# Two key tiles at a time: the TensorE order in the first attention of a four-layer cross-attention kernel

## The chip, the cores and the metric

The kernel runs on one core of one Trainium2 chip. The metric is the device time of one execution in microseconds (us). Before the change it is 2722.48 us, the median of three runs (2721.83 to 2725.4).

## The reference

The program works on a batch of 4 sequences of 256 tokens by 256 features, with a context of 1601 rows by 128 features for each, in four layers: a gated cross-attention with a feed-forward part, a memory layer, a block with self-attention, cross-attention and an expert MLP, and a second memory layer. The change lies in the attention of the first layer, for each of the 4 sequences and 16 heads of width 64:

```
q = (layernorm(x) @ Wq) * 64 ** -0.5          # 256 x 64 for a head
k, v = split(media @ Wkv)                     # 1601 x 64 for a head
sim = where(mask, q @ k.T, -big)              # 256 x 1601
out = softmax(sim) @ v
```

## The kernel before

The kernel is written by hand: every engine has its own program, and semaphores order them. Nothing is scheduled by a planner. An engine takes its instructions strictly in the order of the text, so the order in which the TensorE code is written is the order on the engine.

**The first attention.** Heads are taken in pairs (`p`, 8 pairs for a sequence, called steps here), and keys in 13 tiles of 128 (`kt`, padded from 1601 to 1664). The steps run in a loop that is unrolled twice (steps 0 to 5), with steps 6 and 7 written behind it. In one step TensorE does for each key tile:

- *scores*: four matmuls of 256 columns into a PSUM bank `st` (two banks, taken in turn by `kt % 2`), transposed: keys on the partitions, 2 heads x 256 queries on the free axis. Their operands are high and low halves of float32 numbers (`q_hi_hi`, `k_hi_lo`, `q_lo_shift`, `k_hi_rows`). The scores of tile `kt` wait for the exponential of tile `kt - 2`, which frees the bank (`p_exp`).
- *a maximum part*, `max_part`: softmax needs the maximum of each query over all keys before its scores are computed. For the *next* pair it is taken in 8 parts (2 halves of the keys x 2 heads x 2 query tiles), each two matmuls of 416 columns into PSUM tile `x` (two buffers, `n % 2`). Part `n` waits until VectorE has reduced part `n - 2` (`max_read`). The parts stand at `kt` 2 to 9. The last step of a sequence has no next pair and no parts.
- *the value product*, `pv(kt)`: `v` times the exponentials, for the two heads in the two halves of the array's columns (64 columns each, out of `probs`, into PSUM `pv`). It waits for the exponential of its tile, and it runs two tiles behind the scores.

ScalarE computes the exponentials out of `st` into one of four `probs` buffers (L508). It may write a buffer when the value product and the sums of four tiles before have read it. GpSimd adds the even tiles' exponentials into `prob_sums` (L427 for the first two, L431 for the others), VectorE the odd ones (L1137), both from SBUF. VectorE's program of a step is: two operations that split the weights of a later pair (`w_pair_hi` L1218, `w_pair_lo` L1137), then part 0, the sum of tiles 1 and 3, parts 1 and 2, the sum with tile 5, parts 3 and 4, and so on, each part a `tensor_reduce` over 832 columns of PSUM (L1240). After the 13 tiles TensorE turns the negated maxima (`shifts`, L716), projects queries, keys and values of the pair after next (`prep_q`, `prep_k`, `prep_v`), and adds up the sums.

Nearly all matmuls stand at L623, the helper that records them. They are told apart by their tiles: `st<-q_hi_hi,k_hi_lo` opens the scores of each head, `x<-k_hi_rows,q_hi` is a maximum part, `pv<-probs,v` a value product.

Of the kernel before, what the change touches and what calls it, by code (L numbers as in the profile page):

```python
# [28 lines left out]
KT = -(-S2 // P)  # L29
# [97 lines left out]
def program(nc, io):  # L127

    with ExitStack() as ctx:
# [14 lines left out]
        def sig(name, per=1, primed=False):  # L144
            return Signal(ctx.enter_context(nc.semaphore(name)), per, primed)
# [128 lines left out]
        q_mm, q_hi, q_lo, q_dup = sig("q_mm"), sig("q_hi", 2, primed=True), sig("q_lo", primed=True), sig("q_dup")  # L274
        k_mm, k_hi, k_lo, k_one = sig("k_mm", 2), sig("k_hi", 4), sig("k_lo", 2), sig("k_one", 2)
        v_mm, v_read = sig("v_mm", 4), sig("v_read", 4)
        max_mm, max_read = sig("max_mm", 8), sig("max_read", 8, primed=True)
        nmax, nmax_t, shift_set = sig("nmax"), sig("nmax_t"), sig("shift_set")
# [341 lines left out]
        def _(pe):  # L620
            prime(pe, down_mm, sum_mm, pv_mm, pvs_mm, pvc_mm)
            def mm(out, lhsT, rhs, start=True, stop=True):
                return pe.matmul(out, lhsT, rhs, start=start, stop=stop, skip_group_check=True)  # L623
# [11 lines left out]
            with pe.Fori(0, B) as b:  # L635
# [12 lines left out]
                def prep_q(i, s, p):  # L648

                    pe.wait_ge(w_split.handle, w_split.at(i))  # L650
                    if p == 0:
                        pe.wait_ge(xt_read.handle, xt_read.at(b, 1))
                    if p != 0:
                        pe.wait_ge(q_lo.handle, q_lo.at(i, 0))
                        pe.wait_ge(q_hi.handle, q_hi.at(i, 0))
                    n = 0
                    for ch in range(DC):
                        for w, x in ((whi, xnh), (whi, xnl), (wlo, xnh)):
                            last = mm(MI[:, 0:NT], w[s][:, ch], x[:, ch], n == 0, n == 5)
                            n += 1  # L660
                    last.then_inc(q_mm.handle, 1)

                def prep_k(i, s, p):

                    if p == 0:
                        pe.wait_ge(ctl_ready.handle, ctl_ready.at(b))
                    for j in range(2):
                        if p == 1:
                            pe.wait_ge(k_lo.handle, k_lo.at(i - 1, j + 1))
                            pe.wait_ge(k_hi.handle, k_hi.at(i - 1, 2 * j + 2))  # L670
                        if p is None:
                            pe.wait_ge(max_read.handle, max_read.at(i - 1, 7 + j))
                        for n, (w, x) in enumerate(((whi, cth), (whi, ctl), (wlo, cth))):
                            for ch in range(2):
                                o = j * HALF + ch * QUART
                                last = mm(X[j][:, ch * 512:ch * 512 + QUART], w[s][:, 2], x[:, o:o + QUART], n == 0, n == 2)
                        last.then_inc(k_mm.handle, 1)

                def prep_v(i, s, j, p):

                    if j >= 2:
                        pe.wait_ge(v_read.handle, v_read.at(i, j - 1))
                    elif p == 1:
                        pe.wait_ge(v_read.handle, v_read.at(i - 1, 3 + j))
                    elif p is None and j == 1:
                        pe.wait_ge(shift_set.handle, shift_set.at(i - 1))
                    for kt in range(4 * j, min(4 * j + 4, KT)):
                        o = (kt % 4) * P
                        for n, (w, x) in enumerate(((whi, cth), (wlo, cth), (whi, ctl))):
                            last = mm(ST[j % 2][:, o:o + P], x[:, kt * P:(kt + 1) * P], w[s][:, 3], n == 0, n == 2)  # L690
                    last.then_inc(v_mm.handle, 1)

                def max_part(i, s, n):

                    t = par[s]
                    half, h, qt = n % 2, n // 2 % 2, n // 4
                    if n == 0:
                        pe.wait_ge(q_hi.handle, q_hi.at(i))
                        pe.wait_ge(k_one.handle, k_one.at(i))
                    if n < 2:  # L700
                        pe.wait_ge(k_lo.handle, k_lo.at(i, n + 1))
                        pe.wait_ge(k_hi.handle, k_hi.at(i, 2 * n + 2))
                        pe.wait_ge(max_read.handle, max_read.at(i, 0))
                    else:
                        pe.wait_ge(max_read.handle, max_read.at(i, n - 1))
                    for ch in range(2):
                        o = half * HALF + ch * QUART
                        last = mm(X[half][:, ch * 512:ch * 512 + QUART], t["qx"][:, h, qt * P:(qt + 1) * P],
                                  t["kh1"][:, h, o:o + QUART])
                    last.then_inc(max_mm.handle, 1)  # L710

                def shifts(i):

                    pe.wait_ge(nmax.handle, nmax.at(i))
                    for qt in range(TT):
                        tr = pe.transpose(ST[1][0:2, qt * P:(qt + 1) * P], nmx[:, qt, 0:2], ident)  # L716
                    tr.then_inc(nmax_t.handle, 1)
# [15 lines left out]
                def step(b, p, s, more, last_pair):  # L733
                    i = b * PAIRS + p
                    t = par[s]
                    def pv(kt):
                        pe.wait_ge(p_exp.handle, p_exp.at(i, kt + 1))
                        if kt == 0:
                            pe.wait_ge(norm.handle, norm.at(i, 0))
                            pe.wait_ge(v_read.handle, v_read.at(i))  # L740
                        for h in range(2):
                            r = slice(64 * h, 64 * h + 64)
                            m = mm(PV[r, 0:NT], t["v"][:, kt, r], prob[:, kt % 4, h * NT:(h + 1) * NT], kt == 0, kt == KT - 1)
                        m.then_inc(pv_mm.handle, 1)

                    for kt in range(KT):
                        if kt == 0:
                            pe.wait_ge(k_one.handle, k_one.at(i))
                            pe.wait_ge(k_lo.handle, k_lo.at(i))
                            pe.wait_ge(q_dup.handle, q_dup.at(i))  # L750
                            pe.wait_ge(q_lo.handle, q_lo.at(i))
                            pe.wait_ge(shift_set.handle, shift_set.at(i))
                            if not last_pair:
                                pe.wait_ge(v_read.handle, v_read.at(i + 1))
                        pe.wait_ge(p_exp.handle, p_exp.at(i, max(0, kt - 1)))
                        k = slice(kt * P, (kt + 1) * P)
                        for h in range(2):
                            o = ST[kt % 2][:, h * NT:(h + 1) * NT]
                            mm(o, t["kst"][:, h, k], t["qst"][:, h], True, False)
                            m = mm(o, t["kh1"][:, h, k], t["q2"][:, h], False, True)  # L760
                        m.then_inc(st_mm.handle, 1)
                        if not last_pair and 2 <= kt < 10:
                            max_part(i + 1, 1 - s, kt - 2)
                        if kt >= 2:
                            pv(kt - 2)
                    pv(KT - 2)
                    pv(KT - 1)
                    if not last_pair:
                        shifts(i + 1)
                    if more:  # L770
                        prep_q(i + 2, s, None)
                        prep_v(i + 2, s, 0, None)
                        prep_k(i + 2, s, None)
                    pe.wait_ge(add_pool.handle, add_pool.at(i))
                    pe.wait_ge(add_dve.handle, add_dve.at(i))
                    for h in range(2):
                        for k in range(2):
                            m = mm(PV[64 * h:64 * h + 64, NT:2 * NT], ones[:, 0:64], acc[:, k, h * NT:(h + 1) * NT], k == 0, k == 1)
                    m.then_inc(sum_mm.handle, 1)
                    if more:  # L780
                        for j in range(1, 4):
                            prep_v(i + 2, s, j, None)
                quads(pe, b, step)


# [149 lines left out]
                for j in range(8):  # L935
                    i = b * 8 + j
# [110 lines left out]
                for gr in range(4):  # L1047
                    i = b * 4 + gr
# [50 lines left out]
                for k in range(6):  # L1099
                    i = b * 6 + k  # L1100
# [496 lines left out]
```

## Time and profile before

| | |
|---|---|
| median of three runs | 2722.48 us |
| span of the profiled execution | 2716.7 us |
| median less this span | 5.8 us |
| TensorE matmuls busy | 2181.7 us (80%) |
| VectorE busy | 1527.4 us (56%) |
| ScalarE busy | 866.8 us (32%) |
| GpSimd busy | 466.8 us (17%) |
| mean granted TensorE clock | 0.880 of full |

The page has no time of its own for the profiled execution as a whole. Its span runs from the first to the last instruction, and the median is 5.8 us longer. Busy time of TensorE is the sum of modelled matmuls that overlap each other, so gaps between starts say more than durations.

### The profile page before, as it was taken

What the parts mean: (1) busy time and instruction counts of PE and PEld (TensorE: products, weight loads), DVE (VectorE), ACT (ScalarE), POOL (GpSimd) and SP (SyncE); (2) the same over time, 40 slices, a digit from 0 to 9 for tenths busy, and PEclk for the clock granted to TensorE, in tenths of its full rate; (3) what the DMA queues carried; (4) which work ended last, traced back from release to release, by engine and by line L of the source; (5) the groups of instructions that cost most, each with busy time, mean ns of one, the idle gap of its engine ahead of it and who ended that gap; (6) DMA issues with size and microseconds to landing.
All of it is one profiled execution on the core that took longest, in us unless ns stands there. A gap on an engine that the chain in (4) does not pass through costs nothing.

```text
span 2716.7 us, 37982 instructions
## 1 busy us (share of the span) xinstructions
PE 2181.7 (80%) x12540; PEld 1553.8 (57%) x12540; DVE 1527.4 (56%) x2513; ACT 866.8 (32%) x1530; POOL 466.8 (17%) x412
## 2 busy tenths in 40 slices
PE   4999776887599977688859997768876999776987
PEld 3666565546466665554646665654464665664545
DVE  6676246653666624665367663466437675256643
ACT  2444111451244411144124441205412454120531
POOL 2344010000244401000034440100003443010000
PEclk7999887899699987789969998879897999886988
DMA  4000101001000010100100001010011000101000
GB/s 151 10 7 31 66 1 70 1 1 39 29 9 4 31 66 1 70 1 1 39 29 9 4 31 66 1 70 1 1 40 29 8 4 32 66 1 70 1 1 4
DMA packets 15563, 74.54 MB, mean 27 GB/s; under 512 B 2096, under 2 KB 3760, under 8 KB 11952
## 3 DMA queue, kind: packets, MB, share of 16 engines
q1 hardware_dynamic: 14256, 68.90, 6.9%
q10 hardware_dynamic: 1152, 3.67, 0.3%
q8 instruction: 86, 1.41, 0.2%
q14 instruction: 69, 0.57, 0.1%
HBM read 71.51 MB, written 1.05 MB: 27 GB/s over the span
## 4 chain that ended last, share of the span: by engine, by line
PE 72%; DVE 17%; issue 7%; ACT 3%; DMA 1%; POOL 0%; DVEq 0%; SPq 0%; ACTq 0%; POOLq 0%
PE x L623 25%; PE st L623 22%; PE pv L623 19%; PE mi L623 4%; DVE prob_sums L1420 1%; DVE rstd_work L1137 1%; PE x L642 1%; DVE k_hi_lo L1137 1%; DVE max_parts L1240 1%; DVE recip_sum L1291 1%; DVE cq_blocks L1475 1%; DVE rstd_work L1196 1%; ACT k_hi_lo L466 1%; ACT probs L508 1%; DVE max_parts L1467 1%
## 5 line engine op out<-in xcount | busy, mean ns | idle before, releaser
L508 ACT ACTIVATE probs<-st 128x512 f32<-128x512 f32 x416 | 245.6, 597 | 409.4 <-PE st L623 409.0
L1467 DVE TENSOR_REDUCE max_parts<-x 128x1 f32<-128x832 f32 x256 | 253.7, 1021 | 107.5 <-PE x L623 105.8
L602 ACT ACTIVATE probs<-st 128x512 f32<-128x512 f32 x416 | 226.3, 596 | 184.3 <-PE st L623 181.1
L623 PE MATMUL st<-q_hi_hi,k_hi_lo 128*128 128x256 f32 x832 | 259.2, 334 | 28.9 <-ACT v L474 14.3
L1240 DVE TENSOR_REDUCE max_parts<-x 128x1 f32<-128x832 f32 x256 | 252.3, 1016 | 21.6 <-PE x L623 21.2
L623 PE MATMUL pv<-probs,v 128*64 128x256 f32 x1664 | 258.8, 403 | 0.4
L623 PEld LDWEIGHTS st<-q_hi_hi,k_hi_lo 128*128 128x128 f32 x832 | 159.4, 192 | 166.9 <-ACT probs L508 100.4
L431 POOL TENSOR_TENSOR prob_sums<-prob_sums,probs 128x512 f32<-128x512 f32 x160 | 204.5, 1278 | 290.9 <-ACT probs L508 290.9
L623 PE MATMUL st<-q_lo_shift,k_hi_rows 128*128 128x256 f32 x832 | 218.9, 286 | 0.0
L1137 DVE TENSOR_TENSOR prob_sums<-prob_sums,probs 128x512 f32<-128x512 f32 (+1 forms) x168 | 114.2, 680 | 169.1 <-ACT probs L508 124.6
L395 POOL TENSOR_SCALAR k_hi_rows<-probs,const_cols 64x1664 fp32r<-64x1664 f32 x16 | 26.4, 1659 | 990.2 <-DVE probs L1204 989.9
L623 PE MATMUL st<-cq_blocks,ck_stack 128*128 128x512 f32 x416 | 162.0, 465 | 32.1 <-DVE cq_blocks L1475 30.3
L642 PE MATMUL x<-const_f,x_normed 128*128 128x128 f32 x80 | 22.3, 434 | 200.9 <-DVE x_normed L1172 108.8
L623 PE MATMUL x<-ck_stack,cq_blocks 128*128 128x416 f32 x512 | 154.6, 418 | 29.3 <-DVE cq_blocks L1134 13.7
L1137 DVE TENSOR_TENSOR k_hi_lo<-x,k_hi_lo 64x832 fp32r<-64x832 f32 x128 | 131.0, 1023 | 73.3 <-ACT k_hi_lo L466 71.5
L623 PEld LDWEIGHTS st<-q_lo_shift,k_hi_rows 128*128 128x128 f32 x832 | 161.1, 194 | 0.0
L623 PE MATMUL x<-k_hi_rows,q_hi 128*128 128x416 f32 x512 | 152.7, 385 | 8.2 <-DVE max_parts L1240 5.7
L623 PEld LDWEIGHTS x<-ck_stack,cq_blocks 128*128 128x128 f32 x512 | 107.0, 222 | 62.2 <-issue 31.8
L623 PEld LDWEIGHTS pv<-probs,v 128*64 128x64 f32 x1664 | 86.6, 135 | 92.2 <-issue 61.8
L623 PE MATMUL pv<-probs,v_cross 128*32 128x256 f32 x1664 | 139.1, 392 | 0.0
L623 PEld LDWEIGHTS st<-cq_blocks,ck_stack 128*128 128x128 f32 x416 | 68.6, 194 | 119.0 <-ACT probs L602 80.3
L642 PEld LDWEIGHTS x<-const_f,x_normed 128*128 128x128 f32 x80 | 14.3, 217 | 209.2 <-DVE x_normed L1172 112.3
(260 smaller groups left out, 4387.4 us busy)
## 6 DMA issues: line engine op xcount, KB each, us to landing
w_gate_up<-in_wgu SPq DMA_DIRECT2D x4, 3072.0 KB, 10.4
w_pair<-in_w SPq DMA_DIRECT2D x32, 256.0 KB, 2.7
w_ff<-in_w SPq DMA_DIRECT2D x8, 1024.0 KB, 5.8
w_qk<-in_wqk SPq DMA_DIRECT2D x4, 2048.0 KB, 8.8
w_down<-in_wdn SPq DMA_DIRECT2D x4, 1536.0 KB, 13.7
w_dense<-in_wd SPq DMA_DIRECT2D x4, 1024.0 KB, 11.9
mask_ints<-in_mask SPq DMA_DIRECT2D x4, 832.0 KB, 4.5
ctx_t_raw<-in_ctxT SPq DMA_DIRECT2D x4, 832.0 KB, 6.4
```

The costliest lines, as they stand in the source:

```text
L431: pool.tensor_tensor(acc[:, 0], acc[:, 0], prob[:, (2 * n + 2) % 4], ALU.add)\
L466: act.activation(t["kst"][0:64, h, j * HALF:(j + 1) * HALF].rearrange("p (c n) -> p c n", c=2), X[j][64 * h:64 * h + 64, :].rearrange("p ( ...
L508: act.activation(prob[:, kt % 4], ST[kt % 2][:], ACT.Exp, scale=HD0 ** -0.5).then_inc(p_exp.handle, 1)
L602: act.activation(prob[:, n % 4], ST[n % 2][:], ACT.Exp, scale=float(HC2) ** -0.5)\
L623: return pe.matmul(out, lhsT, rhs, start=start, stop=stop, skip_group_check=True)
L642: last = pe.transpose(X[0][:, o:o + P], src[:, t, ch * P:(ch + 1) * P], ident)
L1137: return dve.tensor_tensor(out, x, y, op)
L1196: link(dve.scalar_tensor_tensor(y, w, 1.5, y, ALU.add, ALU.mult))
L1240: dve.tensor_reduce(mxs[:, qt, h, half:half + 1], X[half][:].rearrange("p (c n) -> p c n", c=2)[:, :, 0:QUART], AX.XY, ALU.max).then_inc(m ...
L1291: dve.reciprocal(rec[:], PV[:, NT:2 * NT]).then_inc(recip.handle, 1)
L1420: link(dve.reciprocal(part, sums))
L1467: dve.tensor_reduce(mxs[:, qt, h, half:half + 1], X[half][:].rearrange("p (c n) -> p c n", c=2)[:, :, 0:QUART], AX.XY, ALU.max).then_inc(m ...
```

## The change

TensorE's program now takes key tiles in twos: scores of two tiles, two maximum parts, two value products. Number, shapes and operands of all instructions stay the same, and so do the conditions on which each waits, except that the waits of the step's start stand ahead of the loop. Other engines' programs are untouched.

```diff
-                    for kt in range(KT):
-                        if kt == 0:
-                            pe.wait_ge(k_one.handle, k_one.at(i))
...
+                    def scores(kt):
                         pe.wait_ge(p_exp.handle, p_exp.at(i, max(0, kt - 1)))
                         k = slice(kt * P, (kt + 1) * P)
                         for h in range(2):
...
                         m.then_inc(st_mm.handle, 1)
-                        if not last_pair and 2 <= kt < 10:
-                            max_part(i + 1, 1 - s, kt - 2)
-                        if kt >= 2:
-                            pv(kt - 2)
-                    pv(KT - 2)
+
+                    pe.wait_ge(k_one.handle, k_one.at(i))
...
+                    for k0 in range(0, KT, 2):
+                        for kt in range(k0, min(k0 + 2, KT)):
+                            scores(kt)
+                        if not last_pair and 2 <= k0 < 10:
+                            max_part(i + 1, 1 - s, k0 - 2)
+                            max_part(i + 1, 1 - s, k0 - 1)
+                        if k0:
+                            pv(k0 - 2)
+                            pv(k0 - 1)
                     pv(KT - 1)
```

On TensorE, in the middle of a step before the change (parts `x`, value products `pv`, scores `st`; a `REGISTER_ALU` prepares a wait):

```order
L705 REGISTER_ALU
L623 MATMUL x<-k_hi_rows_87,q_hi_91 128x416 x2
L623 MATMUL pv<-probs,v_0_82 64x256 x2
L755 REGISTER_ALU
L623 MATMUL st<-q_hi_hi_83,k_hi_lo_80 128x256
L623 MATMUL st<-q_lo_shift_84,k_hi_rows_81 128x256
L623 MATMUL st<-q_hi_hi_83,k_hi_lo_80 128x256
L623 MATMUL st<-q_lo_shift_84,k_hi_rows_81 128x256
```

and the same place after it:

```order
L705 REGISTER_ALU
L623 MATMUL x<-k_hi_rows_87,q_hi_91 128x416 x2
L705 REGISTER_ALU
L623 MATMUL x<-k_hi_rows_87,q_hi_91 128x416 x2
L623 MATMUL pv<-probs,v_0_82 64x256 x4
L747 REGISTER_ALU
L623 MATMUL st<-q_hi_hi_83,k_hi_lo_80 128x256
L623 MATMUL st<-q_lo_shift_84,k_hi_rows_81 128x256
L623 MATMUL st<-q_hi_hi_83,k_hi_lo_80 128x256
L623 MATMUL st<-q_lo_shift_84,k_hi_rows_81 128x256
L747 REGISTER_ALU
```

The second part has moved ahead of the first value product, behind which the second follows at once; four more `st` rows follow, so the engine passes from one kind of work to the next once for two key tiles.

The end of a step on TensorE, before:

```order
L623 MATMUL st<-q_lo_shift_84,k_hi_rows_81 128x256
L623 MATMUL pv<-probs,v_0_82 64x256 x2
L755 REGISTER_ALU
L623 MATMUL st<-q_hi_hi_83,k_hi_lo_80 128x256
L623 MATMUL st<-q_lo_shift_84,k_hi_rows_81 128x256
L623 MATMUL st<-q_hi_hi_83,k_hi_lo_80 128x256
L623 MATMUL st<-q_lo_shift_84,k_hi_rows_81 128x256
L623 MATMUL pv<-probs,v_0_82 64x256 x2
L737 REGISTER_ALU
L623 MATMUL pv<-probs,v_0_82 64x256 x2
L737 REGISTER_ALU
```

and after:

```order
L623 MATMUL st<-q_lo_shift_84,k_hi_rows_81 128x256
L623 MATMUL pv<-probs,v_0_82 64x256 x4
L747 REGISTER_ALU
L623 MATMUL st<-q_hi_hi_83,k_hi_lo_80 128x256
L623 MATMUL st<-q_lo_shift_84,k_hi_rows_81 128x256
L623 MATMUL st<-q_hi_hi_83,k_hi_lo_80 128x256
L623 MATMUL st<-q_lo_shift_84,k_hi_rows_81 128x256
L623 MATMUL pv<-probs,v_0_82 64x256 x2
L737 REGISTER_ALU
L623 MATMUL pv<-probs,v_0_82 64x256 x2
L737 REGISTER_ALU
```

From the scores of the thirteenth tile on nothing has moved, and the first two tiles' scores stood side by side before as well.

## Rows read from the trace of the kernel before

**Rows 1.** The page: the chain that ended last, by engine and by line

```profile
PE 72%; DVE 17%; issue 7%; ACT 3%; DMA 1%; POOL 0%; DVEq 0%; SPq 0%; ACTq 0%; POOLq 0%
PE x L623 25%; PE st L623 22%; PE pv L623 19%; PE mi L623 4%; DVE prob_sums L1420 1%; DVE rstd_work L1137 1%; PE x L642 1%; DVE k_hi_lo L1137 1%; DVE max_parts L1240 1%; DVE recip_sum L1291 1%; DVE cq_blocks L1475 1%; DVE rstd_work L1196 1%; ACT k_hi_lo L466 1%; ACT probs L508 1%; DVE max_parts L1467 1%
```

**Rows 2.** Windows, steps 0, 4, 5, 7: stretch, length, busy, clock, DMA

```profile
69.87:100.24 30.37, 29.77 (x187) 20.85 (x188) 17.47 (x23) 13.93 (x23) 12.05 (x10) 0.92 0.03 10
...
187.19:216.60 29.41, 28.12 (x187) 19.48 (x188) 20.89 (x26) 13.83 (x23) 12.07 (x10) 1.00 0.00 0
216.60:245.40 28.80, 27.83 (x187) 19.40 (x188) 19.82 (x26) 13.82 (x23) 12.29 (x10) 1.00 0.00 0
...
266.58:286.80 20.22, 17.09 (x114) 10.13 (x112) 7.40 (x8) 8.94 (x14) 7.63 (x6) 0.98 0.24 101
```

**Rows 3.** Timeline of TensorE in step 5: start, length, instruction

```profile
217.17 0.28 PE L623 MATMUL st<-q_hi_hi,k_hi_lo 128*128 128x256 f32 x1
217.29 0.28 PE L623 MATMUL st<-q_lo_shift,k_hi_rows 128*128 128x256 f32 x1
...
218.18 0.39 PE L623 MATMUL st<-q_hi_hi,k_hi_lo 128*128 128x256 f32 x1 [0.37 <-ACT probs L508]
...
219.83 0.38 PE L623 MATMUL st<-q_hi_hi,k_hi_lo 128*128 128x256 f32 x1
...
220.41 0.54 PE L623 MATMUL x<-k_hi_rows,q_hi 128*128 128x416 f32 x2
220.88 0.65 PE L623 MATMUL pv<-probs,v 128*64 128x256 f32 x4
221.47 0.39 PE L623 MATMUL st<-q_hi_hi,k_hi_lo 128*128 128x256 f32 x1
...
231.25 0.39 PE L623 MATMUL st<-q_hi_hi,k_hi_lo 128*128 128x256 f32 x1
...
231.92 0.65 PE L623 MATMUL pv<-probs,v 128*64 128x256 f32 x4
```

**Rows 4.** Timeline of TensorE, sums behind step 4: two products in a row

```profile
211.75 1.09 PE L623 MATMUL pv<-prob_sums,const_f 128*64 128x256 f32 x8
212.77 0.33 PE L623 MATMUL st<-w_pair_hi,ctx_t_hi 128*128 128x128 f32 x1
```

**Rows 5.** Timeline of TensorE, later cross-attention: two maximum parts in a row

```profile
561.33 0.93 PE L623 MATMUL x<-ck_stack,cq_blocks 128*128 128x416 f32 x4
562.18 0.64 PE L623 MATMUL pv<-probs,v_cross 128*32 128x256 f32 x8
```

**Rows 6.** Timeline of ScalarE, step 5: first two exponentials

```profile
217.53 1.09 ACT L508 ACTIVATE probs<-st 128x512 f32<-128x512 f32 x2 [1.06 <-PE st L623]
```

**Rows 7.** Timeline of VectorE in step 5

```profile
219.38 0.69 DVE L1137 TENSOR_TENSOR w_pair_lo<-w_pair,w_pair_hi 128x512 fp32r<-128x512 f32 x1
219.99 1.02 DVE L1240 TENSOR_REDUCE max_parts<-x 128x1 f32<-128x832 f32 x1
221.24 0.69 DVE L1137 TENSOR_TENSOR prob_sums<-probs 128x512 f32<-128x512 f32 x1 [0.23 <-ACT probs L508]
221.85 1.95 DVE L1240 TENSOR_REDUCE max_parts<-x 128x1 f32<-128x832 f32 x2
```

**Rows 8.** Timeline of GpSimd in step 5

```profile
219.72 1.50 POOL L427 TENSOR_TENSOR prob_sums<-probs 128x512 f32<-128x512 f32 x1 [3.71 <-ACT probs L508]
223.09 1.28 POOL L431 TENSOR_TENSOR prob_sums<-prob_sums,probs 128x512 f32<-128x512 f32 x1 [1.87 <-ACT probs L508]
```

**Rows 9.** Timeline of all engines, start of step 2 (began at 129.02)

```profile
132.14 1.29 POOL L427 TENSOR_TENSOR prob_sums<-probs 128x512 f32<-128x512 f32 x1 [3.70 <-ACT probs L508]
132.26 1.72 DVE L1137 TENSOR_TENSOR w_pair_lo<-w_pair,w_pair_hi 128x512 fp32r<-128x512 f32 x1
...
133.90 1.01 DVE L1240 TENSOR_REDUCE max_parts<-x 128x1 f32<-128x832 f32 x1
...
134.96 0.65 PE L623 MATMUL x<-k_hi_rows,q_hi 128*128 128x416 f32 x2 [0.32 <-DVE max_parts L1240]
```

More of the change, by code:

```diff
@@ L744, in pv @@
                         m.then_inc(pv_mm.handle, 1)
-                    for kt in range(KT):
-                        if kt == 0:
-                            pe.wait_ge(k_one.handle, k_one.at(i))
[L749 to L754, printed above, removed]
+                    def scores(kt):
                         pe.wait_ge(p_exp.handle, p_exp.at(i, max(0, kt - 1)))
@@ L761, in step @@
                         m.then_inc(st_mm.handle, 1)
-                        if not last_pair and 2 <= kt < 10:
-                            max_part(i + 1, 1 - s, kt - 2)
-                        if kt >= 2:
-                            pv(kt - 2)
-                    pv(KT - 2)
+                    pe.wait_ge(k_one.handle, k_one.at(i))
+                    pe.wait_ge(k_lo.handle, k_lo.at(i))
+                    pe.wait_ge(q_dup.handle, q_dup.at(i))
+                    pe.wait_ge(q_lo.handle, q_lo.at(i))
+                    pe.wait_ge(shift_set.handle, shift_set.at(i))
+                    if not last_pair:
+                        pe.wait_ge(v_read.handle, v_read.at(i + 1))
+                    for k0 in range(0, KT, 2):
[7 more added lines that the diff above has]
+                            pv(k0 - 1)
                     pv(KT - 1)
```

## The prediction

> **What bounds the kernel now.** I read the chain that ended last, then windows of single steps, then each engine's timeline inside a step. TensorE is 72% of the chain, with parts of `x`, `st` and `pv` as its largest lines [rows 1]. A step of the first attention takes 28.8 to 30.4 us, the last of a sequence 20.2 us up to the end of its attention, and from step 1 on the granted clock is 1.00 (2.4 GHz) or nearly so [rows 2]. So the four sequences spend about 4 x 217 = 868 us in these steps. In step 5 TensorE starts the scores of tile 3 at 219.83, the part at 220.41, the value product at 220.88 and the next scores at 221.47, without a recorded wait [rows 3]. The 1.64 us for a tile (3.26 for two) are TensorE's own: here a shorter TensorE sequence shortens the step, until another engine is late.
>
> **What a change of work costs on TensorE.** Within a block of scores, matmuls start 0.12 us apart (217.17, 217.29), so a block of four that continues another costs 0.48; the block behind a value product costs 0.58 (219.83 to 220.41) [rows 3]. Second blocks save 0.10. A part in front of a value product costs 0.47 (220.41 to 220.88) [rows 3]; two in a row of the same shape cost 0.85 (561.33 to 562.18) instead of 0.94 [rows 5], which saves 0.09. A value product costs 0.58 to 0.59 (220.88 to 221.47) [rows 3]; two products of the same shape in a row, those of the sums, cost 1.02 (211.75 to 212.77) [rows 4], which saves 0.145. Together 0.335 us for two tiles: 3.26 becomes 2.925. Where there is no part, scores take 0.67 up to the value product (231.25 to 231.92) [rows 3]: 0.10 of that is entry and 0.09 exit, so with the value product the saving is 0.335 again.
>
> The Trainium skill says, in TensorEngine Tiling (Array Packing), Key Properties, that changing the tiling mode drains the engine while changing tiles does not. Scores and parts are marked 128\*128, value products 128\*64, and in this case's rows the part behind scores starts without an extra gap and the gaps lie on both sides of `pv`. By that rule grouping scores with parts alone would give nothing, and halving the visits to `pv` gives all.
>
> A step has five such pairs (k0 of 2, 4, 6, 8, 10); tiles 0, 1 and 12 keep their order. TensorE's saving is 5 x 0.335 = 1.675 us in each of 32 steps, 53.6 us if nothing else is late.
>
> **What is late next.** I follow one pair, T being the start of its first scores. Second scores at T+0.58, parts at T+1.06 and T+1.44, value products at T+1.91 and T+2.35, next pair at T+2.925. ScalarE takes 1.09 for two exponentials [rows 6] and is no limit; the scores two tiles on want it at T+2.925. VectorE is. It takes an even part, the sum, then the odd part. The even part is ready 0.58 after its start, at T+1.64; the next instruction follows a reduction by 0.93 (1.95 for two less 1.02) and follows a sum by 0.61 [rows 7]. The sum is wanted at T+2.57.
>
> Here a new collision arises. GpSimd's sum began 1.62 us after the scores of its even tile (221.47 to 223.09) and took 1.28 [rows 3, 8]: T+1.62 to T+2.90. Before, VectorE's sum of the odd tile came one TensorE turn later and missed it. Now it lands inside. What such a meeting costs is in two places: `w_pair_lo`, 0.69 us alone, took 1.72 when GpSimd's sum had begun 0.12 before it, and the reduction behind it started at 133.90, 0.47 after GpSimd had ended at 133.43 [rows 7, 9]; and where `w_pair_lo` was first (219.38 to 220.07), GpSimd's sum took 1.50 instead of 1.28 [rows 7, 8]. So the second comer waits for the first. The odd reduction then starts at T+2.90+0.47 = T+3.37, ends at T+4.39, and the odd part of the next pair may start at T+4.43. TensorE wants it at T+2.925+1.44 = T+4.365. It waits 0.07, and a part that waited took 0.65 instead of 0.54 [rows 3, 9]: 0.18 in all, once in two pairs, since the wait gives the next pair its slack.
>
> The skill names this too: GPSIMD Engine Reference, Specifications, says that GpSimd shares its SBUF interfaces with VectorE, with contention when a VectorE instruction has two SBUF inputs. The sums have two, the reductions read PSUM; the trace agrees.
>
> By kind of step, with the start of tile 2's scores as T2:
>
> - Steps 1, 3, 5. The first reduction cannot start before 219.99, T2+1.81 (T2 = 218.18), as VectorE finishes its split first. The sum is wanted at T2+2.74, GpSimd holds on to T2+3.04 (221.22), the odd reduction runs from T2+3.51 to T2+4.53. Part 3 starts at T2+4.57 instead of T2+4.365: 0.2 and 0.11. Later one wait of 0.18. Saving 1.675 - 0.49 = 1.19.
> - Steps 2 and 4. VectorE comes later: first reduction at 133.90, T2+3.30 (T2 is 1.58 behind the step's start, as in step 5). Part 2 may start at T2+4.35 (wanted T2+3.985: 0.37 + 0.11); the odd reduction ends at T2+5.85, so part 3 starts at T2+5.89 against T2+4.85 (1.04 + 0.11). With the later 0.18 these waits are 1.8 us, where before they were 29.41 - 28.80 = 0.61 [rows 2]. Saving 1.675 - 1.8 + 0.61 = 0.5.
> - Step 6 has no split in front; VectorE is free, one wait of 0.18: 1.5.
> - Step 7 has no parts: 1.7.
> - Step 0 runs its first microseconds at the lower clock (0.92 over the step [rows 2]): its first parts come late and gain less. I take 1.4.
>
> A sequence: 1.4 + 3 x 1.19 + 2 x 0.5 + 1.5 + 1.7 = 9.2; four: 37. The work between steps keeps its place relative to the loop's end: the negated maximum is needed 2.1 us after tile 12's scores, while VectorE's last sum, held up by GpSimd, ends about 1.2 after them. The span of 2716.7 becomes about 2680, and with 5.8 around it the time is about 2686. I say 2685.
>
> **Bounds.** If the two sums do not disturb each other, steps 1, 3, 5 wait 0.1, steps 2 and 4 save 0.7, and the total is about 45: 2677. If TensorE also hid those waits, 53.6: 2669. If VectorE set the pace in every pair (2.96 from 4.40 - 1.44, with 0.11 for the exposed weight load 3.07), a pair with parts saves 0.19: 28 x (4 x 0.19 + 0.335) + 4 x 1.7 = 37, less 2 x 4 x 1.2 for steps 2 and 4: 27, or 2695. Outside these steps the clock falls to its lower level in places (mean 0.880), and work that shifts against it can move the total by a few us either way.
>
> **Rivals.**
>
> 1. *The sums do not collide, or harmlessly.* For it: an overlap here is only the last 0.3 us of GpSimd's sum. Against: both rows above. 2677.
> 2. *VectorE sets the pace.* For it: its margin is below 0.1 us in each pair. Against: the loop over two pairs has room. 2695.
> 3. *The switching cost is no switching cost* but belongs to value products whatever stands beside them. For it: ends are modelled. Against: starts are what I used, and [rows 4, 5] show both pairs in place. 2722, no change.
> 4. *Slower: the collision stretches VectorE's sum to a fixed length.* If each sum took 1.72 us from its own start, as `w_pair_lo` did [rows 9], the odd reduction would start at T+4.21 and end at T+5.23; the next odd part at T+5.27 makes a pair 3.83 instead of 3.26. That is 112 x 0.57 = 64 us lost against 28 x 0.335 + 7 = 16 won: 2770. It decides from a pair of 3.40 us, that is when the odd part can't start before T+4.85. Against it: `w_pair_lo` began with GpSimd and ended 0.55 behind it, so it waited and was not slowed.
>
> **How the numbers follow.** Forecast 57%, rival 1 20%, rival 2 13%, rival 3 5%, rival 4 5%. The first three are faster by over 0.2% (5.4 us, about what a measurement can tell from no change): 0.90; same 0.05; slower 0.05. A range from 2671 to 2700 takes in the forecast and rivals 1 and 2 with the clock's few us and leaves out the other two and the full 53.6.
>
> **What would show it.** Two value products in a row should take 1.02, two parts 0.85, eight score matmuls 1.06; a pair in step 5 2.9 to 3.1 us. VectorE's sums should lengthen from 0.69 to 0.9 or so, where GpSimd's overlaps, with short waits of odd parts for `max_parts`; steps 1, 3 and 5 should take 27.6, steps 2 and 4 28.9, step 7 about 18.5 us to 286.80's place. Pairs near 3.4 us, sums of 1.7 us or scores waiting for exponentials would prove me wrong.

## The result and the profile after

The changed kernel takes 2683.41 us (median of four runs, 2678.89 to 2685.0) against 2723.94 us before: a ratio of 0.9847, 95% interval 0.9833 to 0.9861. It is faster by about 41 us. A second set of five runs gave 2685.06 us and 0.9852 (0.9838 to 0.9866). The profiled execution has a span of 2682.2 us. One of the nine executions of the kernel before that were measured beside that second set took 3341 us at a mean clock of 0.611; the ratios leave it out.

The attention of the first layer, from the first scores of a sequence to the output projection behind it, went from 217.52, 218.32, 218.29 and 217.50 us for the four sequences to 207.30, 208.11, 208.10 and 208.15, 40.0 us less in all. Windows of the changed kernel for steps 0, 2, 3 and 7, which answer to [rows 2] (the last window ends where the output projection is about to begin, so I compare step 7 by its scores below):

```profile
69.59:98.39 28.80, 28.20 (x188) 21.79 (x188) 18.54 (x23) 13.51 (x23) 12.05 (x10) 0.92 0.04 11
...
125.85:154.65 28.80, 26.74 (x188) 20.03 (x188) 21.72 (x26) 13.40 (x23) 12.22 (x10) 1.00 0.04 9
154.65:182.10 27.45, 26.44 (x187) 19.97 (x188) 21.03 (x26) 13.29 (x23) 12.24 (x10) 1.00 0.04 10
...
258.00:276.50 18.50, 15.29 (x114) 10.25 (x112) 11.08 (x9) 8.39 (x14) 7.65 (x6) 1.00 0.25 106
```

In the first sequence step 0 fell from 30.37 to 28.80, steps 1, 3 and 5 from 28.80 to 27.46, steps 2 and 4 from 29.4 to 28.80, step 6 from 21.18 to 19.65. The other sequences agree but for step 0: it fell from 31.12 to 29.62 and from 31.18 to 29.59 in the second and third, and only from 30.35 to 29.67 in the fourth. In step 7 the scores of tile 12 start 12.38 us after the step's start instead of 14.30. TensorE in step 3, to be laid beside [rows 3]:

```profile
156.22 0.39 PE L623 MATMUL st<-q_hi_hi,k_hi_lo 128*128 128x256 f32 x1 [0.37 <-ACT probs L508]
...
156.80 0.30 PE L623 MATMUL st<-q_hi_hi,k_hi_lo 128*128 128x256 f32 x1
...
157.30 0.91 PE L623 MATMUL x<-k_hi_rows,q_hi 128*128 128x416 f32 x4
158.14 1.08 PE L623 MATMUL pv<-probs,v 128*64 128x256 f32 x8
159.15 0.39 PE L623 MATMUL st<-q_hi_hi,k_hi_lo 128*128 128x256 f32 x1
...
160.21 1.22 PE L623 MATMUL x<-k_hi_rows,q_hi 128*128 128x416 f32 x4
161.36 1.08 PE L623 MATMUL pv<-probs,v 128*64 128x256 f32 x8
162.37 0.39 PE L623 MATMUL st<-q_hi_hi,k_hi_lo 128*128 128x256 f32 x1
```

The first pair takes 156.22 to 159.15, that is 2.93 us, as 0.58 + 0.50 for eight score matmuls, 0.84 for two parts and 1.01 for two value products. The next, 159.15 to 162.37, takes 3.22: its four part matmuls last 1.22 instead of 0.91, since the odd part waits. The reason stands on VectorE and GpSimd at that place:

```profile
161.73 0.87 DVE L1142 TENSOR_TENSOR prob_sums<-prob_sums,probs 128x512 f32<-128x512 f32 x1
162.52 1.01 DVE L1245 TENSOR_REDUCE max_parts<-x 128x1 f32<-128x832 f32 x1
```

```profile
160.77 1.28 POOL L431 TENSOR_TENSOR prob_sums<-prob_sums,probs 128x512 f32<-128x512 f32 x1 [1.52 <-ACT probs L508]
```

GpSimd's sum begins 1.62 after the pair's scores (159.15) and ends at 162.05. VectorE's sum is issued inside it and ends 0.55 behind it; the reduction starts 0.47 behind it. In the whole trace 148 two-input operations of VectorE (sums and `w_pair_lo`) start while a sum of GpSimd runs, and all 148 end 0.55 us behind it. By the pages, VectorE's running sums grew over the whole program from a mean of 680 ns to 924, with the same count, while GpSimd's stayed at the 1.28 us of [rows 8]:

```profile
L431 POOL TENSOR_TENSOR prob_sums<-prob_sums,probs 128x512 f32<-128x512 f32 x160 | 205.6, 1285 | 250.0 <-ACT probs L508 250.0
...
L1142 DVE TENSOR_TENSOR prob_sums<-prob_sums,probs 128x512 f32<-128x512 f32 (+1 forms) x168 | 155.2, 924 | 75.0 <-ACT probs L528 42.9
```

### The profile page after: what moved, and what is told of

Its sections match the earlier page's. It is cut to its first block, busy times and chain, and to the rows that moved or that the text cites. A ratio compares the mean times of both kernels' runs of the same rounds, so it can differ in the third digit from the quotient of the medians.

```text
span 2682.2 us, 37982 instructions
## 1 busy us (share of the span) xinstructions
PE 2143.2 (80%) x12540; PEld 1575.9 (59%) x12540; DVE 1572.0 (59%) x2513; ACT 851.2 (32%) x1530; POOL 467.2 (17%) x412
## 4 chain that ended last, share of the span: by engine, by line
PE 72%; DVE 17%; issue 7%; ACT 3%; DMA 1%; POOL 0%; DVEq 0%; SPq 0%; ACTq 0%; POOLq 0%
PE x L623 26%; PE st L623 22%; PE pv L623 18%; PE mi L623 4%; DVE rstd_work L1142 1%; DVE prob_sums L1425 1%; DVE max_parts L1245 1%; PE x L642 1%; DVE k_hi_lo L1142 1%; DVE recip_sum L1296 1%; DVE cq_blocks L1480 1%; DVE rstd_work L1201 1%; ACT probs L508 1%; ACT k_hi_lo L466 1%; DVE max_parts L1472 1%
## 5 line engine op out<-in xcount | busy, mean ns | idle before, releaser
L508 ACT ACTIVATE probs<-st 128x512 f32<-128x512 f32 x416 | 229.6, 596 | 385.3 <-PE st L623 380.6
L1472 DVE TENSOR_REDUCE max_parts<-x 128x1 f32<-128x832 f32 x256 | 253.8, 1021 | 109.2 <-PE x L623 107.6
L1245 DVE TENSOR_REDUCE max_parts<-x 128x1 f32<-128x832 f32 x256 | 258.7, 1017 | 54.6 <-PE x L623 53.2
L602 ACT ACTIVATE probs<-st 128x512 f32<-128x512 f32 x416 | 226.3, 596 | 189.0 <-PE st L623 186.4
L623 PE MATMUL st<-q_hi_hi,k_hi_lo 128*128 128x256 f32 x832 | 236.8, 315 | 28.9 <-ACT v L474 14.3
L623 PE MATMUL pv<-probs,v 128*64 128x256 f32 x1664 | 223.2, 393 | 0.0
L623 PE MATMUL st<-q_lo_shift,k_hi_rows 128*128 128x256 f32 x832 | 213.1, 287 | 0.0
L1142 DVE TENSOR_TENSOR prob_sums<-prob_sums,probs 128x512 f32<-128x512 f32 (+1 forms) x168 | 155.2, 924 | 75.0 <-ACT probs L528 42.9
L623 PE MATMUL x<-k_hi_rows,q_hi 128*128 128x416 f32 x512 | 144.3, 398 | 14.2 <-DVE max_parts L1245 11.9
L623 PEld LDWEIGHTS pv<-probs,v 128*64 128x64 f32 x1664 | 101.0, 137 | 77.3 <-ACT probs L508 24.3
```

What stands on the lines that cost most here:

```text
L508: act.activation(prob[:, kt % 4], ST[kt % 2][:], ACT.Exp, scale=HD0 ** -0.5).then_inc(p_exp.handle, 1)
L602: act.activation(prob[:, n % 4], ST[n % 2][:], ACT.Exp, scale=float(HC2) ** -0.5)\
L1142: return dve.tensor_tensor(out, x, y, op)
L1245: dve.tensor_reduce(mxs[:, qt, h, half:half + 1], X[half][:].rearrange("p (c n) -> p c n", c=2)[:, :, 0:QUART], AX.XY, ALU.max).then_inc(m ...
L1472: dve.tensor_reduce(mxs[:, qt, h, half:half + 1], X[half][:].rearrange("p (c n) -> p c n", c=2)[:, :, 0:QUART], AX.XY, ALU.max).then_inc(m ...
```

## The experiments

All ratios are to the kernel before, run beside each on the same chip.

### Where TensorE's saving comes from

**Value products in twos, the rest alternating.** The part follows each tile's scores, inside the loop over the two tiles:

```diff
-                        if not last_pair and 2 <= k0 < 10:
-                            max_part(i + 1, 1 - s, k0 - 2)
-                            max_part(i + 1, 1 - s, k0 - 1)
+                            if not last_pair and 2 <= kt < 10:
+                                max_part(i + 1, 1 - s, kt - 2)
```

> Only the value products stand in twos; scores and maximum part of each tile alternate as before: S, part, S, part, pv, pv. Theory (TensorE pays for passing to and from the value products, and for nothing else): a pair of tiles takes the same 2.925 us as with everything in twos, 0.58 + 0.385 + 0.48 + 0.47 + 0.43 + 0.58, VectorE's sum still meets GpSimd's, and the time is 2683 us within 3. Rival (every passage between kinds of work costs): only the value products' 0.145 us is saved in pairs with parts, 4 x 28 x 0.145 = 16 us, and 0.335 in the others (17 us), less VectorE's waits of old: 2690 to 2697 us.

Measured: 2683.53 us, ratio 0.9846 (0.9832 to 0.9859), the same as the change. TensorE in step 3:

```profile
156.73 0.28 PE L623 MATMUL st<-q_hi_hi,k_hi_lo 128*128 128x256 f32 x1
...
157.22 0.54 PE L623 MATMUL x<-k_hi_rows,q_hi 128*128 128x416 f32 x2
157.69 1.08 PE L623 MATMUL pv<-probs,v 128*64 128x256 f32 x8
158.70 0.39 PE L623 MATMUL st<-q_hi_hi,k_hi_lo 128*128 128x256 f32 x1
```

Scores behind a part cost 0.49 (156.73 to 157.22), as scores behind scores do; the gaps are in front of `pv` and behind it. Putting scores and parts together adds nothing.

The weight loads of the same place (PEld) show what the gaps are:

```profile
157.10 0.31 PEld L623 LDWEIGHTS x<-k_hi_rows,q_hi 128*128 128x128 f32 x2
157.69 0.63 PEld L623 LDWEIGHTS pv<-probs,v 128*64 128x64 f32 x8 [0.28 <-issue]
158.70 0.19 PEld L623 LDWEIGHTS st<-q_hi_hi,k_hi_lo 128*128 128x128 f32 x1 [0.39 <-issue]
```

Behind scores, the load for the part starts 0.12 us ahead of its matmul (157.22), under the matmuls before. On the way to the value products the loads stand still for 0.28 us, on the way back for 0.39, and each starts only together with its matmul. The kernel before shows the same for other operands: 0.28 and 0.39 around the product of the sums in [rows 4], 0.28 and 0.41 around the 128\*32 products of [rows 5]. So it goes with the tiling and not with the operands of this value product.

**Scores and parts in twos, value products alone.**

```diff
-                        for kt in range(k0, min(k0 + 2, KT)):
-                            scores(kt)
...
-                        if k0:
-                            pv(k0 - 2)
-                            pv(k0 - 1)
+                        parts = not last_pair and 2 <= k0 < 10
+                        scores(k0)
+                        if k0 + 1 < KT and (parts or not k0):
+                            scores(k0 + 1)
+                        if k0:
+                            pv(k0 - 2)
+                        if k0 + 1 < KT and k0 and not parts:
+                            scores(k0 + 1)
+                        if parts:
+                            max_part(i + 1, 1 - s, k0 - 2)
+                            max_part(i + 1, 1 - s, k0 - 1)
+                        if k0:
+                            pv(k0 - 1)
```

> The scores of two tiles together and their two parts together, but each value product alone: S, S, pv, part, part, pv; where there are no parts the old order S, pv, S, pv. Theory: as many visits to the value products as before the change, so a pair takes 3.26 us again and the time is that of before, 2724 us within 4 (the gaps lie on both sides of pv). Rival (grouping scores and parts is worth 0.10 + 0.09 us by itself): 112 pairs x 0.19 = 21 us, 2703 us.

Measured: 2719.78 us, ratio 0.9978 (0.9969 to 0.9987). That is 6 us by the medians, a little more than the 4 allowed, and far from the rival's 21.

```profile
162.68 0.39 PE L623 MATMUL st<-q_hi_hi,k_hi_lo 128*128 128x256 f32 x1
...
163.82 0.65 PE L623 MATMUL pv<-probs,v 128*64 128x256 f32 x4
164.41 1.02 PE L623 MATMUL x<-k_hi_rows,q_hi 128*128 128x416 f32 x4
165.36 0.65 PE L623 MATMUL pv<-probs,v 128*64 128x256 f32 x4
165.94 0.39 PE L623 MATMUL st<-q_hi_hi,k_hi_lo 128*128 128x256 f32 x1
```

The pair takes 3.26 us again (162.68 to 165.94). Two parts between two value products cost 0.95 (164.41 to 165.36) instead of 0.85: they now carry the entry that the scores carried. So the count of visits to `pv` decides. What this kernel gains in its trace is 0.1 us in steps 2 and 4, where tile 12's scores start 17.65 instead of 17.76 after the step's start, and 0.05 in steps 1, 3 and 5: 0.4 us for a sequence, 1.6 in all. The rest of the 6 us is not in the trace, whose execution took 2725.61 us. The eleven executions spread from 2716.37 to 2725.61, and those of the kernel before beside them from 2718.63 to 2727.2. Why more of this kernel's were low is open.

**Twos only where there are no parts.**

```diff
+                        parts = not last_pair and 2 <= k0 < 10
                         for kt in range(k0, min(k0 + 2, KT)):
                             scores(kt)
+                            if parts:
+                                max_part(i + 1, 1 - s, kt - 2)
+                                pv(kt - 2)
...
-                        if k0:
+                        if k0 and not parts:
```

> Twos only where there are no maximum parts: tiles 10 and 11 of the first seven steps, and the whole last step of each sequence; elsewhere the order of before. Theory (each halved visit to the value products is worth 0.335 us, and nothing of VectorE's waits stands here): 28 x 0.335 + 4 x 1.9 (the last step went from 14.30 to 12.38 with the change) = 17 us, a ratio of 0.9938 to the kernel before, 2708 us beside 2725. Rival (the gain lives in the pairs with parts, or depends on both): under 8 us.

Measured: 2702.92 us, ratio 0.9936 (0.9918 to 0.9954), 17.4 us by the ratio (12 to 22) and 21 by the medians. In the trace the second and third attentions shrank by 4.3 us each, which makes 17. Steps 1, 3 and 5 take 28.44 instead of 28.80, and step 7's tile 12 starts at 12.40. The saving of 0.335 for a pair adds up.

### Where the rest of the saving went

**Both parts, then the sum, on VectorE.**

```diff
                     for kt in range(KT):
+                        if not last_pair and 2 <= kt < 10:
+                            max_part(i + 1, kt - 2)
                         if kt % 2 and kt > 1:
...
-                        if not last_pair and 2 <= kt < 10:
-                            max_part(i + 1, kt - 2)
```

> The changed kernel, with VectorE's order turned: it reduces both parts of a pair and only then adds the exponentials. Theory (what is missing from the full saving is VectorE's odd part, held up by the sum and by GpSimd's sum inside it): the sum begins at T+3.50, after GpSimd's has ended (T+2.90), and takes 0.69 again; odd parts no longer wait; steps 1, 3, 5 take 0.4 us less, steps 2 and 4 about 0.8 less; in all 10 to 13 us: 2671 us. Rival (the waits are elsewhere, or TensorE has other work that hides them): 2680 us or more.

Measured: 2670.3 us, ratio 0.9799 (0.9785 to 0.9812), 13 us less than the change alone. VectorE in step 3:

```profile
159.68 1.96 DVE L1245 TENSOR_REDUCE max_parts<-x 128x1 f32<-128x832 f32 x2 [0.21 <-PE x L623]
161.55 0.68 DVE L1142 TENSOR_TENSOR prob_sums<-prob_sums,probs 128x512 f32<-128x512 f32 x1
162.59 1.96 DVE L1245 TENSOR_REDUCE max_parts<-x 128x1 f32<-128x832 f32 x2 [0.36 <-PE x L623]
```

The sum takes 0.68 again, VectorE now waits for TensorE, and pairs are 2.92 throughout (part pairs start at 156.18, 159.09, 162.01, 164.92). Steps 3 and 5 take 27.05 (but step 3 of the second and third sequence 28.1, see the last section), steps 2 and 4 28.2. In the traces the four attentions are 9.5 us shorter than with the change alone; the rest of the difference lies in stretches outside them, where the programs are the same.

**GpSimd's sum behind VectorE's.**

```diff
                     for n in range(6):
+                        if n < 5:
+                            pool.wait_ge(add_dve.handle, add_dve.at(i, n + 1))
+                            pool.sem_inc(passed.handle, 1)
```

> The changed kernel, but each of GpSimd's first five sums waits until VectorE's sum of the tile behind has ended, so that the two never meet, and the weight split of steps 2 and 4 meets none either. Theory (the first comer holds the other up): VectorE's sums take 0.69 instead of 0.8 to 0.9, the split 0.69 instead of 1.7; the odd part is ready at T+4.24 before TensorE wants it at T+4.37; steps 1, 3, 5 gain 0.25 us, steps 2 and 4 about 1.1: 2671 us. Rival (two sums that meet cost nothing that matters; the late start of VectorE does): only a few tenths for a sequence, 2681 us or more. If GpSimd's later sums hold up exponentials, it is slower than 2683.

Measured: 2699.04 us, ratio 0.9903 (0.9888 to 0.9918), 16 us slower than the change. The sums did keep apart: VectorE's took 0.68 or 0.69 (but for 13 of 208) and `w_pair_lo` in step 2 took 0.69. But three rows of step 3, from ScalarE, GpSimd and TensorE, show that the last case of the expectation came true, with the first sum already:

```profile
160.51 1.08 ACT L511 ACTIVATE probs<-st 128x512 f32<-128x512 f32 x2 [3.21 <-POOL prob_sums L430]
```

```profile
159.19 1.29 POOL L430 TENSOR_TENSOR prob_sums<-probs 128x512 f32<-128x512 f32 x1 [5.93 <-DVE prob_sums L1145]
```

```profile
163.41 0.65 PE L626 MATMUL x<-k_hi_rows,q_hi 128*128 128x416 f32 x2 [0.37 <-DVE max_parts L1248]
```

The exponential of tile 4 waits until GpSimd has read the buffers of tiles 0 and 2. Its first sum, begun late, holds up the exponential of tile 4 to 160.51; with it come tile 5's and VectorE's sum of it, behind which the odd part's reduction stands. So the run shows that sums which don't meet take their own time, but not what the meeting alone costs.

### The late steps

**The split of later weights behind the negated maximum**, once with the turned order and once without:

```diff
-                    if more:
-                        dve.wait_ge(v_mm.handle, v_mm.at(i))
-                        split(i + 2, s)
                     for kt in range(KT):
...
                         neg_max(i + 1)
+                        if more:
+                            dve.wait_ge(v_mm.handle, v_mm.at(i))
+                            split(i + 2, s)
                         shifts(i + 1, 1 - s)
```

> The changed kernel with the weight split moved behind the negated maximum, VectorE's order as it was. Theory: steps 2 and 4 lose their lateness (28.80 to about 27.2 us, 8 x 1.6 = 13 us) and steps 1, 3, 5 the wait of their first pair (12 x 0.25 = 3 us); the wait of 0.07 and 0.11 us that the meeting sums cause stays: 2668 us. Rival (the meeting sums, not the late start, cost most): 2677 us or more.

> The changed kernel with VectorE's order turned (both parts, then the sum) and the split of later weights moved from the start of the step to behind the negated maximum. Theory (what is left of the waits after turning the order are steps 2 and 4, where the split makes VectorE late): all steps with parts take 27.05 us as steps 3 and 5 did with the turned order, instead of 28.2 in steps 2 and 4: 8 x 1.15 = 9 us less than the 2670 of the turned order: 2661 us. Rival (the split then makes the query projection late, which waits for it): 2668 us or more.

Measured: 2698.36 us, 0.9911 (0.9893 to 0.993), without the turned order; 2692.87 us, 0.9893 (0.9872 to 0.9915), with it. Both miss; the rival named for the second is what happened, in both. The loop itself did as expected: with both, tile 12's scores start 15.41 to 15.49 after the step's start in all of steps 1 to 6, and with the moved split alone 15.6 to 15.7, where the change had 17.16 in steps 2 and 4. (One step 2, at 16.67, is for the last section.) So it was the late start that cost most inside the loop, as the first expectation said. But steps 1 to 5 as a whole take 28.5 and more. With both edits, step 3 ends like this (GpSimd, VectorE, TensorE in order of time):

```profile
175.36 1.27 POOL L431 TENSOR_TENSOR prob_sums<-prob_sums,probs 128x512 f32<-128x512 f32 x1 [0.88 <-ACT probs L508]
175.47 1.71 DVE L1142 TENSOR_TENSOR w_pair_lo<-w_pair,w_pair_hi 128x512 fp32r<-128x512 f32 x1
175.87 0.38 PE L716 MATMUL st<-const_f,neg_max 128*2 128x128 f32 x2
...
177.40 0.38 PE L623 MATMUL mi<-xn_t_hi,w_pair_hi 128*128 128x256 f32 x1 [1.15 <-DVE w_pair_lo L1142]
```

The moved split ran into GpSimd's last sum, took 1.71 us instead of 0.69, and TensorE's query projection waited 1.15 us for it (1.19 in the run without the turned order). It starts 1.54 us after the turned maxima (L716) instead of 0.13, which is the whole loss of 1.4 us for a step. Here the price of the meeting is laid bare: 1.0 us of those 1.4.

**The split where GpSimd is idle**, on top of the turned order:

```diff
-                    if more:
-                        dve.wait_ge(v_mm.handle, v_mm.at(i))
-                        split(i + 2, s)
                     for kt in range(KT):
...
+                        if not last_pair and kt == 9:
+                            neg_max(i + 1)
+                        if more and kt == 9:
+                            dve.wait_ge(v_mm.handle, v_mm.at(i))
+                            split(i + 2, s)
                         if kt % 2 and kt > 1:
...
                     if not last_pair:
-                        neg_max(i + 1)
                         shifts(i + 1, 1 - s)
```

> The changed kernel with VectorE's order turned, the negated maximum right behind the last part (tile 9) and the weight split right behind it, ahead of the sum of tile 9, where GpSimd is idle. Theory (with the split behind the negated maximum the loop already took 15.41 us in every step, and what was lost was 1.0 to 1.2 us in front of the query projection, since the split met GpSimd's last sum): the split takes 0.42 + 0.69, the projection does not wait, all steps 1 to 5 take 27.05 us: 8 x 1.15 us less than the 2670 of the turned order: 2661 us. Rival (VectorE's two remaining sums each meet one of GpSimd's and the shift is late): 2668 us or more.

Measured: 2658.4 us, ratio 0.9755 (0.9741 to 0.9769). This is the fastest version: 67 us under the kernel before beside it, 27 under the change. Of the 67, 59 lie in the four attentions of the traces, and of the 27, 19; the rest lies outside them, where the programs are the same. VectorE in step 3:

```profile
168.13 0.16 DVE L1250 TENSOR_REDUCE neg_max<-max_parts 128x4 f32<-128x8 f32 x1
168.35 0.43 DVE L1223 CAST w_pair_hi<-w_pair 128x512 fp32r<-128x512 f32 x1
168.81 0.69 DVE L1142 TENSOR_TENSOR w_pair_lo<-w_pair,w_pair_hi 128x512 fp32r<-128x512 f32 x1
169.42 3.59 DVE L1142 TENSOR_TENSOR prob_sums<-prob_sums,probs 128x512 f32<-128x512 f32 x2
```

The split takes its own time: it comes first, and GpSimd's sum that starts inside it takes 1.60 us instead of 1.28. The two sums behind it take 3.59 us, as each meets one of GpSimd's, and TensorE waits for none of them. Steps 1, 3, 4 and 5 of the first sequence take 27.05 to 27.09 us.

**VectorE's edits on the kernel before.** Turned order, and the split behind the negated maximum, with the old TensorE order:

```diff
-                    if more:
-                        dve.wait_ge(v_mm.handle, v_mm.at(i))
-                        split(i + 2, s)
                     for kt in range(KT):
+                        if not last_pair and 2 <= kt < 10:
+                            max_part(i + 1, kt - 2)
...
-                        if not last_pair and 2 <= kt < 10:
-                            max_part(i + 1, kt - 2)
...
                         neg_max(i + 1)
+                        if more:
+                            dve.wait_ge(v_mm.handle, v_mm.at(i))
+                            split(i + 2, s)
```

> The kernel before with both changes to VectorE's program and the old TensorE order. Theory (TensorE's sequence set the pace before, and only steps 2 and 4 waited for VectorE, 0.6 us each): 8 x 0.6 = 5 us at most, a ratio of 0.998. Rival (VectorE's program was the pace all along and TensorE's new order only let it run ahead): 30 us or more.

Measured: 2723.78 us, ratio 0.9997 (0.9984 to 1.001). Steps 2 and 4 lost their lateness (tile 12 at 17.17 instead of 17.76), and all steps got 0.1 us or so longer behind the loop, which took back part of it: in the trace the second and third attentions are 0.5 us shorter, 2 us in all, too little to be told from no change. It shows that VectorE's program was not the pace before; it became it only with the new TensorE order.

**The changed kernel again.**

> The changed kernel once more, beside the last variant on the same chip: 2683 us within 3, ratio 0.985.

Measured: 2685.06 us, ratio 0.9852, as told above.

## Why the prediction was right

The forecast was 2685 us with 2671 to 2700; the time is 2683.4.

- *TensorE's terms.* Two value products 1.02 forecast, 1.01 measured; two parts 0.85 and 0.84; eight score matmuls 1.06 and 1.08; a pair 2.925 and 2.93. The price belongs to the way to and from the value products: three runs show it from three sides (all of it without grouping scores and parts, next to none of it without grouping value products, 0.335 us each where nothing else moves). Rival 3, a cost of the value products whatever stands beside them, is out by the same runs. The rule that a change of tiling mode drains the array, in the Trainium skill's TensorEngine Tiling (Array Packing), Key Properties, is borne out: scores and parts alternate at no cost, and it is the passage between 128\*128 and 128\*64 that costs about 0.33 us there and back, with the weight loads held up at both sides.
- *The collision of the sums* came as drawn: GpSimd from T+1.62, VectorE's sum ending 0.55 behind it, the odd part late. The sum grew to between 0.77 and 0.89 in such pairs and to about 1.37 where there are no parts and it is issued earlier. The end is what is fixed (0.55 us behind GpSimd's), not the length: rival 4, a stretch to 1.72, is out. Rival 1 is out too, since the sums did meet and odd parts waited, and so is rival 2: from the third on, pairs with parts take 2.91 to 3.02 in steps 1 to 6, not 3.07 each.
- *The kinds of step.* Steps 1, 3, 5: 1.19 forecast, 1.34 measured; the first wait was 0.3 as worked out, the second 0.10 instead of 0.18. (With the first wait that pair takes 3.22, above the 2.9 to 3.1 that I had named for a pair of step 5.) Steps 2 and 4: 0.5 against 0.6; part 2 was to start at T2+4.35 and part 3 at T2+5.89. In step 2 T2 is 127.43:

```profile
131.78 0.65 PE L623 MATMUL x<-k_hi_rows,q_hi 128*128 128x416 f32 x2 [0.20 <-DVE max_parts L1245]
133.31 0.65 PE L623 MATMUL x<-k_hi_rows,q_hi 128*128 128x416 f32 x2 [0.89 <-DVE max_parts L1245]
```

  That is T2+4.35 and T2+5.88. Step 6: 1.5 against 1.53. Step 0: 1.4, a guess, against 1.57, 1.50, 1.59 and 0.68, a mean of 1.33; that the guess came so near is luck. Step 7: 1.7 against 1.92. There the missing 0.2 is a wait before the first value product of old: the previous step's normalisation, `attn_t`, ended at 268.92, and the product began at 269.02, 0.85 us after the scores of tile 2 (268.17) instead of 0.67. It is now covered by the second scores.
- *The total.* The four attentions shrank by 40.0 us where I had 37, and the medians differ by 40.5. The profiled spans differ by 34.5 only. The 5.4 us between lie outside the attention, 4.7 of them between the third and the fourth. Windows of the kernel before, of the stretch between the second and third attention and of that between the third and fourth:

```profile
962.30:1419.70 457.40, 339.60 (x1769) 248.84 (x1770) 239.95 (x453) 116.72 (x217) 28.31 (x30) 0.82 0.08 30
1637.99:2090.59 452.60, 333.36 (x1769) 243.41 (x1770) 240.20 (x453) 116.39 (x217) 28.31 (x30) 0.84 0.08 31
```

  and of the changed kernel, between the third and fourth:

```profile
1607.09:2064.40 457.31, 339.49 (x1769) 248.66 (x1770) 239.99 (x453) 116.74 (x217) 28.28 (x30) 0.82 0.08 30
```

  The same instructions took 457.40 us at a clock of 0.82 and 452.60 at 0.84 in one execution of the kernel before, and in the traces of all other runs such a stretch took 454.9 to 458.4. So the changed kernel lost nothing there: the profiled execution of the kernel before was fast in this one place. The 5.8 us that I added around the span hold the same difference. In every execution on record the time is about 1.8 us more than the span, so the profiled one took about 2718.5, 4 us less than the median. Adding 5.8 put the forecast back on the median of 2722.5, from where 37 us lead to 2685.5. What the sum had too small is the 3 us that the attentions saved beyond it. That the time is nevertheless only 1.6 us off is in part luck: the median of the kernel before, taken with a fourth run, is 1.5 us higher (2723.94) than the one that I had started from.

Turning VectorE's order confirms the account from the other side: with it, pairs run at TensorE's 2.92. What remained in steps 2 and 4 was the late start, and it went with the split. What the meeting of the sums costs by itself in a pair with parts no run has separated from VectorE's order.

## What to carry to other kernels

Count how often TensorE passes between matmuls of different tiling, not between kinds of work: group those of the odd tiling and leave the others where they help the engines behind. When a faster order moves an engine's work in time, look for the two-input SBUF operations of VectorE and GpSimd that it brings together, since the second waits out the first, and let VectorE do first what frees TensorE's buffers. Price an operation moved out of the way where it lands: the same weight split cost 1.7 us beside GpSimd's sum and 0.69 a few microseconds earlier.

## What the runs showed of the hardware that was not expected

The clock fell to its lower level (1.2 GHz) inside a nearly gapless stretch. In the last variant, windows at the start of step 2 of the first sequence:

```profile
123.40:126.80 3.40, 2.80 (x23) 2.67 (x23) 3.32 (x4) 1.66 (x4) 1.88 (x2) 0.91 0.01 2
126.80:130.00 3.20, 3.20 (x16) 2.91 (x16) 1.52 (x2) 1.82 (x4) 0.00 (x0) 0.56 0.00 0
```

TensorE had been busy for 2.80 of 3.40 us ahead of it, with the usual 0.6 us wait for the value copy in front of the step, and then ran mostly at 1.2 GHz for about 3 us. Step 2 took 28.11 instead of 27.05 us. The other steps of this run have the same wait and kept 1.00 or nearly so. It does not belong to this variant: with the turned order alone, step 3 of the second and third sequence took 28.11 and 28.10 us at a mean clock of 0.94 instead of 27.05, and with the split behind the negated maximum, step 2 of the first sequence took 29.98 and 29.72 at 0.94 instead of 28.5 and 28.7. The second set of runs of the changed kernel shows it in its trace too (step 2 of the first sequence, 0.94), the first does not. I can't say what set it off.
